# Local attention in one transformer block: another order of the stages, and softmax for eight heads at a time

## The reference

```python
h = shift_token(x)                       # half of the channels from the token before
q, k, v = split(h @ wqkv)                # 8 heads of 64
q, k = l2norm(q) * qs, l2norm(k) * ksc
q, k = rotary_xpos(q, k)
sim = einsum('bhwid,bhwjd->bhwij', q * 8, k)    # windows of 64, each with the one before it
attn = softmax(where(mask, -big, sim))
x = x + einsum('bhwij,bhwjd->bhwid', attn, v) @ wo
# then shift_token, layer norm, a gated gelu unit
```

## Time and profile before

| | |
|---|---|
| three runs | 2109.16, 2113.95 and 2114.88 us; median 2113.95 |
| the profiled execution | 2109.33 us, its span 2107.5 us |
| first layer's local attention | from 1088.9 to 1497.6 us of the span |
| second layer's | from 1596.3 to 2006.1 us |
| TensorE, VectorE, ScalarE, GpSimd busy over the span | 85%, 52%, 71%, 23% |

### The profile page before, as it was taken

How to read it: one execution, slowest core, us unless ns; L and a number is a source line. 1 busy time by engine, 2 the same in 40 slices (tenths; PEclk the granted TensorE clock), 3 DMA queues, 4 the chain that set the end, 5 groups by cost and what they waited for, 6 DMA issues and landing times. The chain is left out here.

```text
span 2107.5 us, 67629 instructions
## 1 busy us (share of the span) xinstructions
PE 1795.9 (85%) x28076; PEld 1072.2 (51%) x28076; DVE 1101.3 (52%) x3240; ACT 1491.6 (71%) x2585; POOL 480.6 (23%) x351
## 2 busy tenths in 40 slices
PE   7888999999989999999976777777696777777688
PEld 5664555555555555555534455445332454555433
DVE  5545333333333333333047777776546777777554
ACT  4333999999989999999955667676433666666633
POOL 1104000000000000000027555553005565556100
PEclk9997999999999999999998889898898898898889
DMA  1002111111111111111030000000000000000000
GB/s 53 3 3 74 65 53 54 54 54 53 54 54 55 55 55 55 55 55 39 3 96 16 16 16 22 15 12 10 6 0 18 16 16 16 15 22 10 11 5 35
DMA packets 42327, 69.51 MB, mean 33 GB/s; under 512 B 7376, under 2 KB 33104, under 8 KB 42064
## 3 DMA queue, kind: packets, MB, share of 16 engines
q1 hardware_dynamic: 42064, 65.66, 9.9%
HBM read 21.08 MB, written 2.10 MB: 11 GB/s over the span
## 5 line engine op out<-in xcount | busy, mean ns | idle before, releaser
L653 ACT ACTIVATE x_probs<-x_pss 128x1024 f32<-128x1024 f32 x832 | 806.4, 1021 | 53.7 <-PE x_pss L574 38.8
L588 PE MATMUL x_acc<-x_probs,x_v 128*32 128x256 f32 x6656 | 437.5, 380 | 0.0
L574 PE MATMUL x_pss<-x_qx,x_kx 32*128 32x256 bf16 x9984 | 349.7, 271 | 13.0 <-issue 5.5
L574 PEld LDWEIGHTS x_pss<-x_qx,x_kx 32*128 32x128 bf16 x9984 | 221.9, 93 | 199.5 <-ACT x_probs L653 179.4
L1181 ACT ACTIVATE l_prob<-l_sim,l_neg_top,l_inv_norm 128x128 f32<-128x128 f32 x512 | 245.4, 481 | 27.9 <-DVE l_neg_top L1085 27.8
L967 PE MATMUL l_pst<-w_identity,l_prob 128*128 128x128 f32 x512 | 107.8, 347 | 175.4 <-DVE l_prob L1095 175.3
L588 PEld LDWEIGHTS x_acc<-x_probs,x_v 128*32 128x32 f32 x6656 | 206.6, 110 | 93.1 <-issue 9.0
L871 POOL TENSOR_TENSOR l_turned_half<-l_raw,l_tabB 128x512 f32<-128x512 f32 x128 | 193.3, 1531 | 243.7 <-ACT l_raw L1141 240.5
L700 DVE COPY x_vnext<-x_psp 128x128 f32<-128x128 f32 (+1 forms) x199 | 59.3, 298 | 317.4 <-PE x_psp L552 312.2
L967 PEld LDWEIGHTS l_pst<-w_identity,l_prob 128*128 128x128 f32 x512 | 74.5, 176 | 240.2 <-DVE l_prob L1095 222.8
L880 POOL TENSOR_TENSOR l_direct<-l_direct,l_turned_half 128x1024 f32<-128x1024 f32 x64 | 175.3, 2740 | 70.7 <-DVE l_direct L1045 67.9
(11 more groups left out here) (166 smaller groups left out, 2663.3 us busy)
## 6 DMA issues: line engine op xcount, KB each, us to landing
x_kx<-x_kp SPq DMA_DIRECT2D x96, 208.0 KB, 2.3
x_cT<-in_context SPq DMA_DIRECT2D x16, 832.0 KB, 4.5
x_qx<-x_qp SPq DMA_DIRECT2D x48, 192.0 KB, 2.8
l_vmid<-l_vt SPq DMA_DIRECT2D x64, 128.0 KB, 2.3
xT<-in_x SPq DMA_DIRECT2D x8, 256.0 KB, 5.1
shifted<-zT SPq DMA_DIRECT2D x32, 64.0 KB, 2.0
out_x<-xT SPq DMA_DIRECT2D x8, 256.0 KB, 2.0
shifted<-zT SPq DMA_DIRECT2D x32, 63.8 KB, 2.0
```

The source lines that it names most:

```text
L574: ins = pe.matmul(pss[bank(k, 2 * p + r // 2)][:, r % 2, e, :], kx[par][rows, g, j * P:(j + 1) * P], qx[par][rows, g, a * S:(a + 1) * S], ...
L588: ins = pe.matmul(acc[32 * r:32 * r + 32, 0:S], v[:, j, g, r, :], probs[SLOT[p]][r // 2][:, r % 2, e, :], start=(u == 0), stop=(u == UNITS ...
L653: act.activation(probs[SLOT[p]][y][:, :, :, :], pss[bank(k, 2 * p + y)][:, :, :, :], ACT.Sigmoid, scale=HD ** -0.5).then_inc(weighed, 1)
```

## The change

`mask`, `exps`, `norm`, `turn_over` and `copy` lose their argument h and handle all eight heads of a tile of queries at once. `pst` is one buffer of two banks in place of two of one. Waits are counted anew (two for each element, where there were four). The order of all four engines is another: the last part of an element's work (`norm` and `turn_over` of its second tile, its copy, `value`, `copy_out`) is done in the turn after its own; `project_v`, `copy_v`, `roots`, `inverse_norms` and `scale_keys` are a turn later than they were, `project_v` and `copy_v` in the element's own turn, the other three one turn ahead of it.

```diff
-        pst = [ps(f"pst{h}", [P, HALF, P]) for h in range(2)]
+        pst = ps("pst", [P, FH, P])
...
             def turn(x):                          # GpSimd
                 for t in range(2):
+                    scale_keys(later(x, 1), t)
+                for t in range(2):
                     turn_halves(later(x, 2), t)
                     join(later(x, 2), t)
-                for t in range(2):
-                    scale_keys(later(x, 2), t)
...
-            def turn_over(x, b, h):
+            def turn_over(x, b):
                 if exists(x):
                     n, r, _ = x
-                    pe.wait_ge(normed, 4 * n + 2 * b + h + 1)
-                    at_least(pe, copied, 4 * n + 2 * b + h - 1)
-                    for m in range(HALF):
-                        ins = pe.transpose(pst[h][:, m, :], prob[b][:, HALF * h + m, :], w["identity"][:, :])
+                    pe.wait_ge(normed, 2 * n + b + 1)
+                    at_least(pe, copied, 2 * n + b)
+                    for m in range(FH):
+                        ins = pe.transpose(pst[:, m, :], prob[b][:, m, :], w["identity"][:, :])
                     ins.then_inc(turned, 1)
...
             def turn(x):                          # TensorE
                 project_qk(later(x, 2), 0)
+                turn_over(later(x, -1), 1)
+                project_v(x, 0)
+                project_qk(later(x, 2), 1)
+                value(later(x, -1), 1)
+                project_v(x, 1)
+                score(x, 1)
+                flip(later(x, 1), 0)
                 project_out(later(x, -1))
-                turn_over(x, 0, 0)
-                project_qk(later(x, 2), 1)
-                turn_over(x, 0, 1)
-                score(x, 1)
+                turn_over(x, 0)
+                flip(later(x, 1), 1)
                 value(x, 0)
-                flip(later(x, 1), 0)
-                project_v(later(x, 1), 0)
-                turn_over(x, 1, 0)
-                flip(later(x, 1), 1)
-                turn_over(x, 1, 1)
-                project_v(later(x, 1), 1)
                 score(later(x, 1), 0)
-                value(x, 1)
...
                     dve.wait_ge(v_projected, 2 * n + t + 1)
+                    at_least(dve, valued, 2 * n - 2)
                     dve.tensor_copy(vt[r % 2][:, t, :], psvy[:, :]).then_inc(v_ready, 1)
...
-            def norm(x, b, h):
+            def norm(x, b):
                 if exists(x):
...
-                    dve.tensor_tensor(prob[b][:, at, :], prob[b][:, at, :],
-                                      inv_total[b][:, at].unsqueeze(2).broadcast_to([P, HALF, P]), ALU.mult).then_inc(normed, 1)
+                    dve.tensor_tensor(prob[b][:, :, :], prob[b][:, :, :],
+                                      inv_total[b][:, :].unsqueeze(2).broadcast_to([P, FH, P]), ALU.mult).then_inc(normed, 1)
...
             def turn(x):                          # VectorE, after
+                norm(later(x, -1), 1)
+                mask(x, 0)
+                inverse_norms(later(x, 1))
+                copy_v(x, 0)
+                straight_part(later(x, 2), 0)
+                copy_v(x, 1)
+                sums(later(x, 2), 0)
+                norm(x, 0)
+                mask(x, 1)
+                place_keys(later(x, 1), 0)
+                place_keys(later(x, 1), 1)
+                straight_part(later(x, 2), 1)
+                sums(later(x, 2), 1)
+                add(later(x, -1))
+                floor_of(later(x, 2))
...
             def turn(x):                          # ScalarE, after
+                roots(later(x, 1))
+                copy_qk(later(x, 2), 0)
+                copy(later(x, -1), 1)
+                exps(x, 0)
+                squares(later(x, 2), 0)
+                copy_qk(later(x, 2), 1)
+                copy_out(later(x, -1), 1)
+                place_queries(later(x, 1), 0)
+                copy(x, 0)
+                place_queries(later(x, 1), 1)
+                exps(x, 1)
+                squares(later(x, 2), 1)
+                copy_out(x, 0)
```

More of the change, by code:

```diff
@@ L977, in value @@
                     at_least(pe, o_ready, 2 * n + b)
[L978 to L986, removed]
+                    pe.wait_ge(copied, 2 * n + b + 1)
+                    for p in range(PH):
+                        for k, (_, _, first, last) in enumerate(KEYS[b]):
+                            for e in range(2):
+                                at = slice((2 * p + e) * FD, (2 * p + e + 1) * FD)
+                                v = vt[r % 2][:, 0, at] if b == 0 else (vmid[r % 2][:, at] if k == 0 else vt[r % 2][:, 1, at])
+                                ins = pe.matmul(pso[64 * e:64 * e + 64, p, first:last], v,
+                                                probT[b][:, 2 * p + e, first:last], start=True, stop=True)
                     ins.then_inc(valued, 1)
@@ L1064, in inverse_norms, with mask @@
                     dve.wait_ge(newton, 4 * n + 3)
[L1065 removed]
+                    at_least(dve, exped, 2 * n - 2)
                     dve.scalar_tensor_tensor(inv_norm[r % 2][:, :, :], tmp_b[:, :, :], 1.5, root[:, :, :], ALU.add, ALU.mult).then_inc(newton, 1)
[L1068 removed]
+            def mask(x, b):
                 if exists(x):
                     n, r, _ = x
[L1072 to L1074 removed]
+                    c = 2 * n + b
+                    dve.wait_ge(scored, c + 1)
+                    at_least(dve, exped, c - 1)
                     dve.memset(beat[:, :], 0.0)
[L1076 removed]
+                    for head in range(FH):
                         ins = dve.tensor_tensor_reduce(out=sim[b][:, head, :], in0=pss[head % 2][:, head // 2, :],
@@ L1105, in turn @@
             def turn(x):
-                mask(x, 0, 0)
-                mask(x, 0, 1)
-                norm(x, 0, 0)
-                add(later(x, -1))
-                straight_part(later(x, 2), 0)
-                norm(x, 0, 1)
-                mask(x, 1, 0)
-                mask(x, 1, 1)
-                sums(later(x, 2), 0)
-                straight_part(later(x, 2), 1)
-                norm(x, 1, 0)
-                copy_v(later(x, 1), 0)
-                place_keys(later(x, 1), 0)
-                sums(later(x, 2), 1)
-                norm(x, 1, 1)
+                norm(later(x, -1), 1)
[11 more added lines that the diff above has]
+                sums(later(x, 2), 1)
+                add(later(x, -1))
                 floor_of(later(x, 2))
-                place_keys(later(x, 1), 1)
-                copy_v(later(x, 1), 1)
-                inverse_norms(later(x, 2))
             for tab, const, scales in ((tabA, "cosine", "scales"), (tabB, "sine", "scales_turned")):
@@ L1172, in copy_out, with exps @@
                     act.activation(oT[:, :, b * P:(b + 1) * P], pso[:, :, :], ACT.Copy).then_inc(o_ready, 1)
-            def exps(x, b, h):
+            def exps(x, b):
                 if exists(x):
                     n, r, _ = x
-                    c = 4 * n + 2 * b + h
+                    c = 2 * n + b
                     act.wait_ge(negated, c + 1)
-                    at_least(act, turned, c - 3)
-                    for head in range(HALF * h, HALF * h + HALF):
+                    at_least(act, turned, c - 1)
+                    for head in range(FH):
                         ins = act.activation(prob[b][:, head, :], sim[b][:, head, :], ACT.Exp,
```

32 lines of the change are left out of this document (8 added, 24 removed).

## The result

| | before | changed |
|---|---|---|
| median | 2111.55 us (4 runs, 2105.11 to 2114.88) | 2142.71 us (4 runs, 2136.58 to 2147.97) |
| ratio | 1 | 1.0150, 95% interval 1.0111 to 1.0189 |
| the profiled execution | 2109.33 us, span 2107.5 | 2144.53 us, span 2142.7 |
| first layer's local attention | 408.7 us | 422.5 us |
| second layer's | 409.8 us | 421.1 us |

What follows compares the result with a forecast made beforehand. No engine is full; the order in which engines wait for each other sets the time. Per layer 18.1 +0.3 -1.8 +3.0 = 19.6 us, 39.2 for two, on 2109.33: 2148.5, said as 2150, range 2076 to 2172.

Steps and rivals of the forecast that it cites:

- The walk: One steady turn of the new orders followed step by step across the engines: 25.3 us where it took 23.91.
- 13 x 1.39 = 18.1: Full turns of local_attention in one layer: 13 turns, each 1.39 us longer, add 18.1 us.
- Turn 14: Turn with no element to prepare: 18.1 us against 19.9, so -1.8 a layer.
- the last stretch: End of each layer's local attention, with an extra turn at the slow clock: 25.6 us against 22.6, +3.0.
- rival D: As the walk, and TensorE's clock falls ahead of the flip too: 22 us more, 2172; chance 0.15.
- The low clock at `turn_over`: TensorE, after 4.9 us idle, runs turn_over(x-1,1) at the low clock: eight transposes take 1.94 us against 1.09.
- The walk's bound: VectorE's first norm: 0.2 us of delay loses its place and costs the whole join; from there to 11.0 delay is free.
- Two of the prediction's signs: In the profile after: norm's product 2.4 us long for b = 0, and sums waiting for squares twice.
- The blocking theory: VectorE instructions with two SBUF inputs and GpSimd's block each other, the later waiting; norm(x,0)'s product waits 1.15 us.
- `sums` ahead of the norm: In VectorE's order, norm(x,0) waits behind sums(x+2,0) though its exponentials are ready at 6.9: costs 2 to 3 us.
- `exps(x,1)` stood idle behind `place_queries`: ScalarE starts exps(x,1) at 17.23, queued behind place_queries(x+1,1), though its negated maxima were there at 14.90.
- a saving of fixed cost: Eight heads at a time save about 0.17 us each, four times a turn, two of them on the path.

Runs made afterwards that it cites:

- the run with four idle matmuls: Changed kernel with four idle matmuls of 512 columns on TensorE ahead of turn_over(x-1,1): 2124.91 us, ratio 1.0048.
- the run with nine: Changed kernel with nine idle matmuls of 512 columns on TensorE ahead of turn_over(x-1,1): 2168.92 us, ratio 1.0260.
- the wait of the join alone: Changed kernel with only GpSimd's first join waiting until norm(x,0) is done, no work left out: 2108.80 us, ratio 0.9977.
- the short join: Changed kernel with GpSimd's join for the first tile cut from 16 to 1 of the 16 heads of q and k: 2113.73 us, ratio 1.0004.
- the swap: Changed kernel with exps(x,1) ahead of place_queries(x+1,1) in ScalarE's order: 2080.14 us, ratio 0.9849.
- the new orders: Changed kernel's orders with the five functions handed on four heads at a time, as in the kernel before: 2173.59 us, ratio 1.0285.
- the old ones: Changed functions, eight heads at once, in the orders of the kernel before: 2287.05 us, ratio 1.0812.
- the better orders: Two versions of the changed kernel built from the experiments, with several steps reordered: 2044.42 us and 2036.03 us.
- The last kernel: 2044.42 us version without the join's wait, sums(x+2,1) and floor_of a turn later, roots, inverse_norms, scale_keys and others moved: 2036.03 us, ratio 0.9639.
- a better order: Changed kernel with norm(x,0), then place_keys(x+1,0), ahead of sums, project_out behind the second flip, first join waiting for norm(x,0): 2044.42 us, ratio 0.9686.

## Why the prediction was right, by its steps

**The chain.** The walk and the turn shown above, with t from the end of the norm's product:

| | walked | measured |
|---|---|---|
| ScalarE's copy begins | 2.04 | 2.07 |
| product of norm(x,0) arrives | 9.87 | 9.28 |
| the join | 8.68 to 11.02 | 8.29 to 10.65 |
| that product ends | 12.23 | 11.73 |
| negation of mask(x,1) ends | 14.90 | 14.12 |
| second flip begins | 15.6 | 14.86 |
| exps(x,1) ends | 21.09 | 20.27 |
| norm(x,1) ends | 25.3 | 24.63 |

Each link holds. The first 0.4 us of the difference is GpSimd's: `scale_keys` began 0.14 us earlier, `straight_part` and the two halves behind it took another 0.25 less than walked, and the end of the join passes the shift on to all that follows. The rest is 0.1 to 0.3 us here and there, of both signs.

**The terms of the sum.** The term that was mis-sized most is 13 x 1.39 = 18.1. Measured are 322.06 - 310.78 = 11.3 us in the first layer and, from 1673.37 to 1994.34, 320.97 - 310.93 = 10.0 in the second: 24.73 a turn. Turn 14 was -1.6 (said -1.8), the last stretch 26.45 - 22.6 = +3.8 (said +3.0), the start +0.2 in the first layer (said +0.3). With these the first layer's sum is 13.8, and the two layers together cost 25.0 us where I said 39.2. The turn of 24.73 is an average in which rival D has a part: ahead of the second `flip` the clock falls in six of the 26 turns (1.80 to 1.94 us for 1.06) and partly in three more, 6 us in all. The medians differ by 31 and the profiled executions by 35: the rest lies outside `local_attention`, 6.7 us of it ahead of the first layer (1095.60 against 1088.86). In other runs with the same code in front, the first layer begins anywhere from 1087 to 1098, so I take that for the scatter of one execution; it wasn't tested. That the median came within 7 us of 2150 is in part luck: the sum was 14 us too high for the two layers, and the 6 to 10 us from outside them, for which it had no term, made up for some of that.

**The clock.** The low clock at `turn_over` was right in this turn (1.97 us, after 4.47 idle) and in 17 others of 26, not in all. Its price was not the 0.9 us that it adds: the seven turns at the high clock are no shorter (24.69 against 24.72), and the run with four idle matmuls got 18 us back, which is about that of six turns in which the norm was in time. The walk's bound, that a delay between the join's start and its end is free, is borne out by the changed kernel itself, where the product arrives at 8.36 to 10.82 and ends at 11.5 to 12.2. In the run with nine the product comes behind that bound, at 11.4, and there the delay costs 0.9 us of turn.

Two of the prediction's signs didn't hold in every turn: the product for b = 0 takes anything from 1.22 to 3.36 us and not 2.4, by when it meets the join, and `sums` mostly waits for `squares` once a turn and not twice. The path that they were to show is right.

**What the norm waits for.** The blocking theory is shown by the wait of the join alone (-34 us) and by the short join (-29): both take 0.8 us off an average turn. That `sums` ahead of the norm costs is shown only where the join is out of the way or in the turns in which the product is in time. That `exps(x,1)` stood idle behind `place_queries` is shown by the swap, -63, the dearest of the lines that were tried by themselves.

**What the prediction didn't see.** I called the handing of eight heads a saving of fixed cost. It is worth 31 us in the new orders, and in the old ones, as written here, it costs 173. The times of the products (72 us against 46 in a stretch that differs by 21) say that most of the 31 is GpSimd holding one product once and two halves twice; no run isolates this from the fixed cost saved. The two parts of the change can't be judged one at a time.

**Left open.** No run tests whether a later `turned_half`, or `copy_v(x,1)` behind the norm, brings the better orders down to their walks. The last kernel's join still holds the norm.

## What to carry to other kernels

When an order is written by hand, walk one turn with the time at which each step's inputs are ready beside the time at which it is reached; the difference is what the order costs, and here a swap of two lines was worth 63 us and one wait 34. Two engines that block each other need an order too: let the one that is off the path wait for the one that is on it. A change that puts a step within some tenths of a microsecond of another engine's long instruction makes a gain that comes in some turns and not in others, so give it room or a semaphore.

## What the runs showed of the hardware

A negation of eight columns by VectorE takes 0.17 us alone, 0.73 when it comes during a join (in the run with the join's wait alone) and 0.65 during a `turned_half` (in the changed kernel): even so small an instruction with two SBUF inputs waits for the rest of a long one of GpSimd. An arrival 0.02 us after the start of a join of 2.36 us cost a product 2.2 us (3.42 against 1.22). Between two GpSimd instructions that follow each other without a wait VectorE's waiting one goes first: in the changed kernel a pair of `turned_half` takes 3.49 us when a VectorE product gets in like this and 2.50 without. It has to be there in time: a negation that came 0.02 to 0.04 us before a join's end, in 12 turns of the run called a better order, let the `turned_half` go first and took 1.28 us.
